# Another order of steps on five engines, and one wait of TensorE moved

## The chip, the cores and the metric

The kernel runs on one core of a Trainium2 chip. The metric is the time of one execution on the device in microseconds (us). The kernel before takes 4313.2 us, the median of three runs (4311.36 to 4319.83 us). On a core five engines work side by side, each through its own stream of instructions: TensorE (PE in the profile, with its weight loads as PEld), VectorE (DVE), ScalarE (ACT), GpSimd (POOL) and SyncE (SP), which here issues the DMAs. They wait for one another by semaphores.

## The reference

The input is 64 sequences of 256 steps with 80 features. `h` holds 252 x 128 values for each:

```python
h = tok(x)                        # taps -2..2 of 80 features -> 128, bias, relu, batch norm over all tokens
h = h + attn0(layernorm(h))       # 8 heads of 16, softmax, +0.1 within 5 steps of the diagonal
h = h + ffn0(layernorm(h))        # 8 experts of 256, exact gelu, the top 2 of a softmax gate
h = h + attn1(layernorm(h))       # linear attention: elu+1 features, causal sums, values of 64
h = h + ffn1(layernorm(h))        # layer norm, causal softmax attention (2 heads, l2 norm), then
                                  # 8 experts of 512, tanh gelu, weighted by a softmax gate
```

All in 32-bit floats; for most products the kernel splits both factors into two 16-bit halves and takes three products for one.

## The kernel before

The 64 sequences are worked in 32 pairs; a pair is 504 tokens, in four tiles of 126. A first stage computes the taps of all pairs and the statistics of the batch norm, and stores the result of each pair in DRAM. After it the pairs go one after the other through the four layers. Their work is cut into steps, written as generators, one per engine and part; a `yield` ends a step, and many steps are empty on a given engine:

- `q` (`softmax_queries_and_keys`, 7 steps): batch norm, layer norm, queries, keys and values of the first attention; queries and keys go to DRAM and come back scattered. q.3 holds the first turn on TensorE (L1378).
- `a` (`softmax_attention`, 32 steps): scores (a.0 to a.7), turn of the maxima (a.8, L1422), scores again and values (a.9 to a.19), projection, layer norm, gate logits, turn of the gates (a.29, L1361) and the product with the output bias (a.30, L1367).
- `l` (`linear_and_causal_attention`, 48 steps): layer norm, turn (l.2, L1346), query and key projection (l.3, L1301 to L1303), values (l.5 to l.7), then l.8 to l.20 with the products of keys and queries (L1543) and those with the values (L1561), turns and projection (l.21 to l.25), turn (l.28, L1346), projection to queries, keys and values (l.29, L1301 to L1303), turn (l.32, L1603), scores (l.33, l.34), turns and values (l.36 to l.40, L1630 and L1641), projection, gate, turn of the gates (l.46, L1361) and bias product (l.47, L1367). On ScalarE l.4 computes the exponentials (L808); on SyncE l.4 sends the terms to DRAM (L457, L461) and scatters them back (L467, L473).
- `h` (`hidden`): one hidden chunk of 128 units of an expert layer: three products on TensorE (L1301 to L1303, 504 columns), the gelu on ScalarE (L886), a cast on VectorE (L1266), the low half on GpSimd (L660). A pair has 16 chunks in the first expert layer and 32 in the second.
- `o` (`output`): the product of a chunk with the second weights, twelve on TensorE (128 columns each), and the weighted sum on VectorE (L1285).

`run_rounds` (L217) sets the order: a start, 30 rounds and an end. Round r holds `a` of pair r+1, `l` of pair r, `q` of pair r+2, the chunks 4 to 31 of the second expert layer of pair r-1, the 16 of the first expert layer of pair r+1, the first four of the second of pair r, and the outputs that belong to them. For each engine and each of start, round and end a string of letters (L159 to L193) says which part takes its next step; `in_order` (L211) walks through it. A string holds 201 letters for the start, 183 for a round and 172 for the end. All semaphore waits stand in the steps, so an engine meets them in the order of its string. The program is unrolled.

TensorE waits once for the small loads (`small_loaded`: bias tables and vectors) ahead of the first step (L1341).

Of the kernel before, what the change touches and what calls it, by code (L numbers as in the profile page):

```python
# [20 lines left out]
TILES = 4  # L21
# [121 lines left out]
def halves_before(kind, p):  # L143
# [15 lines left out]
SP_START = ("qqqqqqqhhhhaaaaaaaaaaaaaaaaaaaaaaaaaaaaaohhaaoalhhqqqooqohohhhqqqhhaaaaaahaaoololhaooaalllolaaaa"  # L159
          "alloooolallllallaaaaaaalllhhaaoaaaaahlollllollqqhhololoqqlhlhlllhlhhhqllhoolllllhqhoohloolhlqool"  # L160
          "lhohholhl")
SP_ROUND = ("lohoholhhllahaaloaolhohhaooaalllllllhohohhhahlaaalolaahhohllolaaolaoohhlaalohlalaoaahalhhhaaooal"
          "hhooalllqhohohhohllolaaaaoloooohhlqqqhhhoahoohohqlholllololqhlhlhhlohholoqloolohhooooll")
SP_END = ("lllllloohlhlohllhlolllooollhhhhooohlhollohllohhhhohlhlllllhhhhohoohhhllohoolllloooolhllllllllhlo"
          "ohlhoolhohhhhhlhhhoolhoooloohhhoohoooooohohhhoooohhhhohhhhohhhohoooooooooooo")
POOL_START = ("qqqqqqqaaaaaaaaaaaaaaaaaaaaaaaaaaaaahhhhhahhhahaqqhqqhhhhhhoqqoqaaaaalalaoolaaoallaolalalalaalal"
          "aaaloololaalaaallllhaaaooalllolohooolhllaoaallolqqhhholhoollllohqlllqhhhhohoohlhlllohqqlohlllloo"
          "hqooholhl")
POOL_ROUND = ("ollhhhllhaloaahaaolhalhllaloahaloaahhahooahlolhallllaahoaahhohaaaahhohloaholohlalahholaallooooll"
          "hqooohlhhlloohoohlolooohooloaaahololhoohhhoallhqqqhhhloohllhlaoolhhhlohloohlolqhqooqlll")  # L170
POOL_END = ("llhllloolhoooooohhlhlhhollllollllllohoolohhllhhhlholllhllhohoohhoholloooolllohhohlolllhhllolllho"
          "hhhhhhhhohhooohoololoooohlhhooohholhholholoohhhhhhohoohhohohhhhooooolohooooo")
# [7 lines left out]
DVE_START = ("qqqqqqqaaaaaaaaaaaaaaaaaaaaaaaaaaaaoaahhhhhaoahqhhqoooohqhqhhooqqoohhoqohhoooolaaaaaallaalllaala"  # L180
          "lallalaaallalaaaallaalllaalaaaallaahaholqlhlllhholqllhhlooolohllhlhqqlhooolllllholhoqohlhqolollh"
          "qhohholhl")
DVE_ROUND = ("laohalohhoalooohloalllhhoahoahohalahallolohhaoollaalohlhlhhalaahllaololhhaaooaalaoahlhaaoholhhoo"
          "olhoalhlaaohqhholhollaoahoaoolhahoolhlohlollqhollqqhholollhahlooqqhlohqloolhhlohhoohlhl")
DVE_END = ("lhlhhohlollollohlohoololohhlhloollllhlohhlolhohlhlllllolhlhoohllooholohollhholohlllhhlollhoolloo"
          "oolhhlllolohhoholhhhlhohooohhhooohhhoooohhhhhoooohhohohhohhhoooohhoohhohoooo")
# [27 lines left out]
def run_rounds(queries_and_keys, first_attention, second_attention, hidden, output, orders):  # L214

    start, middle, end = orders
    last = PAIRS - 1  # L220
# [12 lines left out]
    in_order(end, {
        "l": second_attention(last), "h": each(hidden, chunks_of(1, last - 1)[LAG:] + chunks_of(1, last)),
        "o": each(output, chunks_of(1, last - 1) + chunks_of(1, last))})


def program(nc, x_dram, w_dram, vec_dram, row_dram, b2_dram, out_dram):
    y_dram = nc.dram_tensor("y_scratch", (PAIRS, 128, TOK), F32, kind="Internal").ap()
    term_dram = [nc.dram_tensor(f"terms{i}", (4, 128, TOK), F16, kind="Internal").ap() for i in range(2)]  # L240
    with ExitStack() as ctx:
# [3 lines left out]
        def sem(name):  # L245
            return ctx.enter_context(nc.semaphore(name))
# [117 lines left out]
        small_loaded = sem("small_loaded")  # L364
# [35 lines left out]
        def _(sp):  # L400
# [138 lines left out]
        def _(pool):  # L539
# [128 lines left out]


        @block.scalar  # L670
        def _(act):
# [206 lines left out]
            def hidden(kind, p, c):  # L878
                _, before = chunks_before(kind, p)
                half = halves_before(kind, p)  # L880
                bias = (V_B0, V_B1)[kind] + c
# [4 lines left out]
                nc.scalar.activation(hid[:, c % HIDS], pf[:, c % 2, 0:TOK], func,  # L886
                                     bias=vec[:, bias:bias + 1]).then_inc(F["hid_ready"], 1)

            def output(kind, p, j):
                pass  # L890

            run_rounds(softmax_queries_and_keys, softmax_attention, linear_and_causal_attention, hidden, output,
                       (ACT_START, ACT_ROUND, ACT_END))


        @block.vector
        def _(dve):
# [374 lines left out]
            def output(kind, p, j):  # L1272
# [5 lines left out]
                if m == per - 1:  # L1278
# [5 lines left out]
                    for i in range(TILES):  # L1284
# [5 lines left out]
            run_rounds(softmax_queries_and_keys, softmax_attention, linear_and_causal_attention, hidden, output,  # L1290
                       (DVE_START, DVE_ROUND, DVE_END))


        @block.tensor
        def _(pe):
# [100 lines left out]
            def softmax_attention(p):  # L1396
# [277 lines left out]
            def output(kind, p, j):  # L1674
# [9 lines left out]
                for i in range(TILES):  # L1684
# [60 lines left out]
```

## Time and profile before

| | us |
|---|---|
| median of three runs | 4313.2 |
| run around the profiled execution | 4319.83 |
| span of the profiled execution | 4319.1 |
| TensorE busy | 4066.8 |
| VectorE busy | 3367.6 |
| ScalarE busy | 2784.5 |
| GpSimd busy | 2596.6 |

The span is that of one execution as the hardware profiler saw it. Busy time counts an engine's own instructions, without waits. Products on TensorE overlap: each takes longer than the time between two starts, so starts are what counts for a run of them. Times in a time line are from the span's start. A bracket behind an instruction gives the time for which its engine was idle before it and the instruction that ended this.

### The profile page before, as it was taken

How to read it: one execution, taken by the hardware profiler on the slowest of the kernel's cores; microseconds unless marked ns; L12 is line 12 of the kernel's file. 1: busy time of each engine (PE TensorE's matmuls, PEld its weight loads, DVE VectorE, ACT ScalarE, POOL GpSimd, SP SyncE). 2: the span in 40 equal slices, each digit the busy share in tenths (PEclk: the TensorE clock that was granted, in tenths of full speed). 3: DMA queues.
4: the chain of work that ended last, by engine and by line, in shares of the span. 5: the costliest groups of instructions: out<-in, count | busy, mean ns of one | idle time of the engine just before them, and what ended most of it. 6: DMA issues, size and time to landing. Idle time of an engine off the chain costs nothing.

```text
span 4319.1 us, 104773 instructions
## 1 busy us (share of the span) xinstructions
PE 4066.8 (94%) x41344; PEld 3009.8 (70%) x41344; DVE 3367.6 (78%) x8878; ACT 2784.5 (64%) x4796; POOL 2596.6 (60%) x2494
## 2 busy tenths in 40 slices
PE   7678999999999999999999999999999999999998
PEld 3346777777777777777777777777777777777766
DVE  3357888888888888888888888878888887888876
ACT  3235766666676666667666666766666676666654
POOL 2034666666666666666666666666666666666656
PEclk9779999999999999999999999999999999999999
DMA  4200000011100001110000111000101100010000
GB/s 149 68 27 28 18 18 29 28 30 30 30 19 24 22 28 30 30 30 18 23 23 28 30 30 30 23 26 16 30 28 30 30 23 26 16 30 28 28 16 6
DMA packets 136939, 127.62 MB, mean 30 GB/s; under 512 B 28928, under 2 KB 135360, under 8 KB 136448
## 3 DMA queue, kind: packets, MB, share of 16 engines
q1 hardware_dynamic: 136448, 120.91, 9.6%
q8 instruction: 328, 5.37, 0.5%
q14 instruction: 163, 1.34, 0.1%
HBM read 71.05 MB, written 49.55 MB: 28 GB/s over the span
## 4 chain that ended last, share of the span: by engine, by line
PE 56%; DVE 24%; ACT 6%; POOL 5%; issue 4%; DMA 3%; SPq 2%; ACTq 0%; DVEq 0%; POOLq 0%
PE pf L1301 9%; PE pf L1303 8%; PE pf L1302 8%; PE pa L1561 8%; DVE h L1285 4%; PE pa L1447 3%; DVE hid_hi L1266 3%; PE pa L1543 3%; PE pa L1346 2%; PE pa L1433 2%; POOL inv_norm L650 2%; PE pa L1301 2%; ACT xn L726 2%; PE pa L1641 2%; PE pa L1303 2%
## 5 line engine op out<-in xcount | busy, mean ns | idle before, releaser
L660 POOL TENSOR_TENSOR hid_lo<-hid,hid_hi 128x504 f16<-128x504 f32 x1536 | 1835.5, 1212 | 775.8 <-DVE hid_hi L1266 775.8
L886 ACT ACTIVATE hid<-pf,vec 128x504 f32<-128x504 f32 x1536 | 1014.7, 680 | 505.5 <-PE pf L1303 356.9
L1301 PE MATMUL pf<-w_hi,hid_hi 128*126 128x128 f16 x6144 | 1133.7, 224 | 10.7 <-DVE h L1285 10.2
L1303 PE MATMUL pf<-w_hi,hid_lo 128*126 128x128 f16 x6144 | 1115.8, 221 | 0.0
L1302 PE MATMUL pf<-w_lo,hid_hi 128*126 128x128 f16 x6144 | 1115.4, 221 | 0.0
L1301 PEld LDWEIGHTS pf<-w_hi,hid_hi 128*126 128x126 f16 x6144 | 844.1, 137 | 153.5 <-issue 53.2
L1302 PEld LDWEIGHTS pf<-w_lo,hid_hi 128*126 128x126 f16 x6144 | 843.8, 137 | 28.5 <-issue 0.2
L1266 DVE CAST hid_hi<-hid 128x504 f16<-128x504 f32 x1536 | 845.4, 573 | 8.2 <-ACT hid L886 2.7
L1303 PEld LDWEIGHTS pf<-w_hi,hid_lo 128*126 128x126 f16 x6144 | 845.2, 138 | 0.0
L1285 DVE SCALAR_TENSOR_TENSOR h<-pf,gates,h 126x128 f32<-126x128 f32 x2048 | 574.1, 342 | 155.2 <-PE pf L1303 152.6
L616 POOL TENSOR_TENSOR pt<-pt,band 126x262 f32<-126x262 f32 x512 | 351.2, 707 | 527.6 <-ACT pt L773 527.4
L1301 PE MATMUL pf<-xf_hi,w_hi 128*128 128x504 f16 x1536 | 582.1, 379 | 8.3 <-ACT hid L886 3.0
L1302 PE MATMUL pf<-xf_lo,w_hi 128*128 128x504 f16 x1536 | 578.8, 377 | 0.0
L1303 PE MATMUL pf<-xf_hi,w_lo 128*128 128x504 f16 x1536 | 578.8, 377 | 0.0
L773 ACT ACTIVATE pt<-pa 126x504 f32<-126x504 f32 x512 | 274.7, 589 | 212.3 <-PE pa L1433 211.7
L1561 PE MATMUL pa<-v,pt 126*126 126x65 f32 x3072 | 382.4, 274 | 1.1 <-DVE o L1167 0.9
L1561 PEld LDWEIGHTS pa<-v,pt 126*126 126x126 f32 x3072 | 361.0, 191 | 2.4 <-issue 2.3
L1069 DVE TENSOR_REDUCE minus_max<-pa 126x2 f16<-126x504 f32 x512 | 325.9, 681 | 20.7 <-PE pa L1409 16.6
L886 ACT ACT_TABLE_LOAD x217 | 278.4, 1283 | 6.8
L1303 PEld LDWEIGHTS pf<-xf_hi,w_lo 128*128 128x128 f16 x1536 | 150.3, 98 | 178.0 <-issue 2.2
L1177 DVE TENSOR_TENSOR pt<-pa,causal 126x504 f32<-126x504 f32 x256 | 173.5, 678 | 94.6 <-PE pa L1543 93.3
L1301 PEld LDWEIGHTS pf<-xf_hi,w_hi 128*128 128x128 f16 x1536 | 152.7, 99 | 125.0 <-issue 41.2
(208 smaller groups left out, 7486.8 us busy)
## 6 DMA issues: line engine op xcount, KB each, us to landing
qk_spread<-terms SPq DMA_DIRECT2D x224, 126.0 KB, 2.5
qk_spread<-terms SPq DMA_DIRECT2D x192, 63.0 KB, 2.3
y_scratch<-hid SPq DMA_DIRECT2D x32, 252.0 KB, 2.1
y_in<-y_scratch SPq DMA_DIRECT2D x32, 252.0 KB, 3.2
terms<-qk_hi SPq DMA_DIRECT2D x32, 252.0 KB, 2.5
terms<-qk_lo SPq DMA_DIRECT2D x32, 252.0 KB, 2.6
qk_spread<-terms SPq DMA_DIRECT2D x32, 252.0 KB
terms<-ot_hi SPq DMA_DIRECT2D x32, 252.0 KB, 2.4
```

The source lines that it names most:

```text
L616: nc.gpsimd.tensor_tensor(strip, strip, band[0:TILE], ALU.mult).then_inc(S0["p_band"], 1)
L660: nc.gpsimd.tensor_tensor(hid_lo[:, c % 8], hid[:, c % HIDS], hid_hi[:, c % 8], ALU.subtract).then_inc(hid_lo_done[c % 2], 1)
L773: nc.scalar.activation(pt[0][0:TILE, i % 8], pa0[0:TILE, i % 2, 0:TOK], ACT.Exp, scale=HEAD ** -0.5).then_inc(S0["p_exp"], 1)
L886: nc.scalar.activation(hid[:, c % HIDS], pf[:, c % 2, 0:TOK], func, bias=vec[:, bias:bias + 1]).then_inc(F["hid_ready"], 1)
L1069: nc.vector.tensor_reduce(minus_max[0:TILE, 2 * b:2 * b + 2, hd // 2, 64 * (hd % 2) + MAX_ROW], pa0[0:TILE, i % 3, 0:TOK].rearrange("p (t ...
L1177: nc.vector.tensor_tensor(pt[1][0:TILE, i % 4].rearrange("p (t q) -> p t q", t=4), pa1[0:TILE, 0, 0:TOK].rearrange("p (t q) -> p t q", t=4 ...
L1266: nc.vector.tensor_copy(hid_hi[:, c % 8], hid[:, c % HIDS]).then_inc(F["hid_hi_done"], 1)
L1285: last = nc.vector.scalar_tensor_tensor(h[0:TILE, i], pf[0:TILE, 2, i * D:(i + 1) * D], gates[0:TILE, kind, i, e:e + 1], h[0:TILE, i], ALU ...
L1301: nc.tensor.matmul(out, ah, bh, start=start, stop=False, skip_group_check=skip)
L1302: nc.tensor.matmul(out, ah, bl, start=False, stop=False, skip_group_check=skip)
L1303: return nc.tensor.matmul(out, al, bh, start=False, stop=stop, skip_group_check=skip)
L1561: last = nc.tensor.matmul(pa1[0:TILE, 1, first:first + wide], factors[:, cols(blk)], v1[0:TILE, 2 * b + kt, hd], start=(t == 0), stop=(t = ...
```

## The change

The fifteen strings are replaced by others with the same number of each letter; so every engine takes the same steps, and the steps of each part in the same sequence, but mixed otherwise. The strings of TensorE and ScalarE for a round are shown; those of SyncE, GpSimd and VectorE, and of start and end, change in the same way. TensorE's wait for the small loads moves into `gate_bias2`, in front of the bias product of pair 0 of either layer.

```diff
-ACT_ROUND = ("lhaaohahloaalhlolhhholhahlolahhoalahooaallllooaoahohlllhhhooolaolloaallaahohaalhoalhhhlahaoalhao"
-             "lhohhhoollhooolohoaooalqaaahhalhhlhhllhlolooolooqqqoooloahlllhqloooohhqloohhlqlhholhhll")
+ACT_ROUND = ("aaahhloooahlaloloohhlhhaoohaololoahhaoolhllhhaalllahoalhlholhalllooaqhaahlahaaholoolhoalahhlhaoa"
+             "hqlloaholhqholoooaoohlhaoaloahhaoohohlhllohloolaohllqooolhlhhlqhlhloqoholqhlhlhoolloalh")
...
-PE_ROUND = ("lhhoalhhaoaoloahlohloaoohlhhlaooahlahohalolhalahllaaoolahollhholallhhalaaolaoloahhaolahhlhoohaoo"
-            "laahlhhlaohaoohlolqhoohalolaaohaoohhhoqqqlholhalhloqlolhlolollhhlooqlhhqololhhoohhoolll")
+PE_ROUND = ("lhhalohoaohaloahlohololhqhahhoaloalohahholalhoaloalalaohloolholhalallhhalhalaoalhhaooahlahaholho"
+            "aloqoalhohhooalohqhlalaooaoolhahohahllohoholhlolhlqohlololhlhaqlohlqholqoholhoolhlholol")
...
@@ -1338,7 +1338,6 @@
             pe.wait_ge(w_lo_done, PIECES)
-            pe.wait_ge(small_loaded, 32 + 16 * TILES)
...
             def gate_bias2(a, p):
+                if p == 0:
+                    pe.wait_ge(small_loaded, 32 + 16 * TILES)
                 pe.wait_ge(SS[a]["gate_t_ready"], n(p + 1))
```

Read out, with capital H and O for the second expert layer of the pair before and small h and o for the first of the next pair, parts of TensorE's round are these. The beginning was `l.0 H4 H5 O0 a.0 l.1 H6 H7 a.1 O1 a.2 O2 l.2 O3 a.3 H8 l.3` and is `l.0 H4 H5 a.0 l.1 O0 H6 O1 a.1 O2 H7 a.2 l.2 O3 a.3 H8 l.3`. Up to l.8 it was `H14 O10 H15 a.8 l.8` and is `O9 H14 a.7 H15 H16 O10 l.8 a.8`. Around l.28 it was `l.25 H30 H31 l.26 a.25 O24 h0 a.26 O25 O26 h1 l.27 O27 l.28 q.0 h2 O28 O29 h3 a.27 l.29` and is `l.25 H30 O24 H31 h0 O25 O26 a.25 l.26 O27 h1 q.2 h2 l.27 a.26 l.28 a.27 O28 O29 a.28 O30 O31 l.29`. Up to l.32 it was `O30 l.30 a.28 a.29 O31 h4 a.30 o0 o1 h5 h6 h7 o2 q.1 q.2 q.3 l.31 h8 o3 l.32` and is `h3 a.29 h4 o0 h5 a.30 h6 l.30 l.31 o1 h7 o2 h8 o3 l.32`. The end was `o13 H2 H3 o14 o15 l.45 l.46 l.47` and is `H2 l.45 H3 o14 l.46 o15 l.47` (here H2 and H3 are of the present pair). On ScalarE the steps up to the exponentials were `H7 l.3 O2 l.4 H8` and are `H7 H8 l.4 H9`.

## Rows read from the trace of the kernel before

**Rows 1.** The page: span; then busy time, share and instructions of each engine

```profile
span 4319.1 us, 104773 instructions
...
PE 4066.8 (94%) x41344; PEld 3009.8 (70%) x41344; DVE 3367.6 (78%) x8878; ACT 2784.5 (64%) x4796; POOL 2596.6 (60%) x2494
```

**Rows 2.** Table by stretches: width; five busy times from PE to POOL; PEclk; DMA

```profile
164.00:280.00 116.00, 64.71 (x491) 38.22 (x493) 51.51 (x148) 32.80 (x59) 38.04 (x43) 0.66 0.10 30
280.00:405.00 125.00, 102.33 (x819) 71.09 (x819) 76.02 (x213) 60.43 (x115) 43.20 (x47) 0.82 0.08 22
...
2291.40:2416.60 125.20, 121.44 (x1276) 91.53 (x1275) 103.04 (x277) 85.79 (x148) 80.41 (x79) 1.00 0.10 27
...
4173.00:4319.00 146.00, 124.77 (x1246) 92.44 (x1243) 90.34 (x205) 66.55 (x115) 78.64 (x66) 0.98 0.05 14
```

**Rows 3.** Time line of POOL: marks of the first and the last round

```profile
405.22 0.62 POOL L631 COPY h<-h 126x512 f32<-126x512 f32 x1
...
4170.81 0.62 POOL L631 COPY h<-h 126x512 f32<-126x512 f32 x1
```

**Rows 4.** Time line of PE: end of one round, then l.2 and l.3

```profile
2287.35 0.28 PE L1361 MATMUL pa<-ident,gates 126*128 126x126 f32 x1
2287.98 1.15 PE L1367 MATMUL pa<-b,gate_t 128*126 128x128 f32 x8 [0.35 <-ACT gate_t L736]
2288.97 0.38 PE L1301 MATMUL pf<-xf_hi,w_hi 128*128 128x504 f16 x1
...
2290.24 0.22 PE L1301 MATMUL pf<-w_hi,hid_hi 128*126 128x128 f16 x1
...
2290.87 0.22 PE L1303 MATMUL pf<-w_hi,hid_lo 128*126 128x128 f16 x1
...
2295.14 0.65 PE L1346 MATMUL pa<-ident,xn 126*128 126x126 f32 x4
2297.42 0.38 PE L1301 MATMUL pa<-xt_hi,w_hi 128*128 128x504 f16 x1
```

**Rows 5.** Time line of PE at a.8 and l.8

```profile
2313.84 0.39 PE L1422 MATMUL pa<-ident,minus_max 126*128 126x126 f16 x4 [0.34 <-DVE qk_spread L1075]
2314.07 0.39 PE L1543 MATMUL pa<-qk_spread 128*126 128x126 f16 x4
```

**Rows 6.** Time line of SP: the last scattering DMA of l.4

```profile
2311.31 0.61 SPq L467 DMA_DIRECT2D qk_spread<-terms  x1
```

**Rows 7.** DMA issues of the page: count, KB each, microseconds to landing

```profile
qk_spread<-terms SPq DMA_DIRECT2D x224, 126.0 KB, 2.5
```

**Rows 8.** Time line of PE at l.28, l.29 (first, last), l.32 and l.37

```profile
2367.46 0.65 PE L1346 MATMUL pa<-ident,xn 126*128 126x126 f32 x4 [0.69 <-ACT xn L726]
...
2371.12 0.38 PE L1301 MATMUL pa<-w_hi,xt_hi 128*126 128x384 f16 x1 [0.36 <-DVE xt_lo L1199]
...
2373.25 0.33 PE L1303 MATMUL pa<-w_hi,xt_lo 128*126 128x384 f16 x1
...
2382.97 1.08 PE L1603 MATMUL pa<-ident,v 126*128 126x126 f32 x8 [0.18 <-DVE v L1215]
...
2392.15 0.54 PE L1630 MATMUL pa<-ident,pt 126*126 126x126 f32 x3 [0.77 <-ACT fs L861]
```

**Rows 9.** Waits of PE over the span: total, times, longest

```profile
PE pa L1543 <- DMA qk_spread<-terms: 9.3, 14, 1.1
```

**Rows 10.** The page's groups: busy, mean ns, idle before

```profile
L886 ACT ACT_TABLE_LOAD x217 | 278.4, 1283 | 6.8
```

**Rows 11.** Time line of ACT at an exponential and a gelu

```profile
2322.89 1.07 ACT L773 ACTIVATE pt<-pa 126x504 f32<-126x504 f32 x2 [0.28 <-PE pa L1433]
2323.98 1.28 ACT L886 ACT_TABLE_LOAD   x1
```

**Rows 12.** Time line of DVE at the operand of the first turn

```profile
166.63 0.54 DVE L1036 TENSOR_SCALAR pt<-y_in,bn_scale,bn_shift 128x504 f32<-128x504 f32 x1 [1.64 <-DMA y_in<-y_scratch]
```

**Rows 13.** Time line of PE at the first turn

```profile
168.97 1.09 PE L1378 MATMUL pa<-ident,pt 128*126 128x128 f32 x4 [7.88 <-DMA b<-in_b]
```

More of the change, by code:

```diff
@@ L156 @@
 SPREAD0, SPREAD1 = 6 * 16, 9 * 16
[L159 to L172, printed above, removed]
@@ L173 @@
-ACT_START = ("qqqqqqqaaaaaaaaaaaaaaaaaaaaaaaaaaaaoaohhhoaohaaqhhqqhhqhhhohholhqqqaaaaahhlalaalalllaalaallloaal"
-          "aalaaaoalaalaooollllaalahhloaooaoaaalhooqqllllhhhololhlllhhlooqqholloholhlloolllhlohlqlooqhlhllq"
-          "hoohholhl")
-ACT_ROUND = ("lhaaohahloaalhlolhhholhahlolahhoalahooaallllooaoahohlllhhhooolaolloaallaahohaalhoalhhhlahaoalhao"
-          "lhohhhoollhooolohoaooalqaaahhalhhlhhllhlolooolooqqqoooloahlllhqloooohhqloohhlqlhholhhll")
-ACT_END = ("hhlhhoollolllohhhooolholllhllolohhlllolohlhoohoohllhlollollhloohloohololohlhohlhloohlhllhloooolo"
-          "llolhlhllllolhhlhoooooohhohhhhhhhohhhoolhhohohoohhoohhhooohhohhohoohohoooooh")
@@ L180 @@
[L180 to L186, printed above, removed]
@@ L187 @@
-PE_START = ("qqqqqqqaaaaaaaaaaaaaaaaaaaaaaaaaaaahhhhaahoaahohhqqoqoqhhoohhhhoolooqqhhqoolooooaaaaaalaalllalaa"
-          "laalalalallaalaaalallllaaalaahlhhlaaaaallollhohllhhlqqhhollqlhqooohlhllqhlhololllloolhoolqholoqh"
-          "llohholhl")
-PE_ROUND = ("lhhoalhhaoaoloahlohloaoohlhhlaooahlahohalolhalahllaaoolahollhholallhhalaaolaoloahhaolahhlhoohaoo"
-          "laahlhhlaohaoohlolqhoohalolaaohaoohhhoqqqlholhalhloqlolhlolollhhlooqlhhqololhhoohhoolll")
-PE_END = ("lhlhhhoohlllolhohoooohollhlhllollohlhllhhlolhlolhllhllolllhohoohlloooloolhhholhhhollolollhhllllo"
-          "ololoololhhllhhlhohhohohohhooohhohhooohohhohhooohhhoohohohhhoooohhhhoooooooo")
+SP_START = ("qqoqaaaohqqaahhlqaaahaallqaaaqqaqhaaaahoaaahhhaoahaahhoqahlahaoqaaqahaaqlllolaaolloaaloaaaaoaaao"
+            "hallqohoooaahllaalhalqaalaloqalaoaalahholaoohlhlllaaoloahhhhlqalllhhoallllhlhlqoqollllolllohlhlq"
+            "olhloohho")
@@ new lines @@
+SP_ROUND = ("lhlahaooaahooaollooolhaaooloalohlhlalhlllhhalhahohhaolllolaaalaaqlalahhhalaoaollhlohaollhoqhhaha"
+            "ahollhoohohhooloooolqlhhllhlohahahllhoolaqhhhoaohohhhlaolqhhqqhhhooloohallllolooloooloh")
+SP_END = ("hllhhohloholhlohlllloloolhloollhhlllohohhloolhhhhlhhohohloolhllllllllhhoollhohllhllolooohoololoo"
+          "olhlhlhlolhhloohohhhloohohhhllohhooooohhooohohhhhohooooohohhhoooohhooohooohh")
+POOL_START = ("qoqqqqqaqaaaaaaaaaaaaaaaaaaaqaaahahhhaqahqhhahhhqahhhoahhhqallaaqaaaooalllalalalaalaaqlaoaoaoaao"
+              "aooloalaloqaalalllloaaqahllllaoolhlolaoqhlhloalhloaohohhllhlhqhllqlalllholaqlhoqhhhoahohllllolol"
+              "olhoooolh")
@@ new lines @@
+POOL_ROUND = ("loloaalholhhaoaaohaalholhhalhohqlolhlloaallahohaolhaaoohahohlllaahalhhlohoolalaaolhhooaooallhhqh"
+              "loolooholhhaoololhhlaaolholhlahhhhlholoollqqhlllhooqalhqhoaaahhlllololhoqhhoooooalolhho")
+POOL_END = ("llohlolohlohoolholllhllhohlllhohhlhhllhlolhloolooooohlhllllllooolhhholhollololhhlloohhohhhhoohhh"
+            "loolhlhlolhlhlhoooooohhhoolohlhloohooooooolhholhhohoohhhhooohoohhohohooohhhh")
+ACT_START = ("aaqqaaqqaqoqaqaaaaaaaaaaaaaaaaaqaaaahqhaohhhlhaahhhhqahaqhqhoaqhhqhaoallaallalloolaaalaaaoaaalao"
+             "llaloaqoaaaaallaoolaollqlaahhllqoholohllllaaahohhlololooohallhahhlhllholqollohllqlhqolllqhololhh"
+             "ollhhoolo")
@@ new lines @@
+ACT_ROUND = ("aaahhloooahlaloloohhlhhaoohaololoahhaoolhllhhaalllahoalhlholhalllooaqhaahlahaaholoolhoalahhlhaoa"
+             "hqlloaholhqholoooaoohlhaoaloahhaoohohlhllohloolaohllqooolhlhhlqhlhloqoholqhlhlhoolloalh")
+ACT_END = ("hloollloohollhlhohhhllhlhlooolhlhhohlolohololohloollolhlloolhllhhlololohllhoohhlohloooholhollllh"
+           "llhllololhoohohollhlhhohlhooohohohohoohoohoohohhhohhooohohhhoohhooohhohhohoh")
+DVE_START = ("qqqqqqqaaaaaaaaaaaaaaaaaaaaaoaaaaqaaqaqhhhahhaahoohhohqohoohoqhqhoohaoqhoohooaolaalalalllllaalaa"
+             "aaalaaalaoalllaaaaqallqalaalalaaalahllllhhlhlalhhlholoohlhallolhqhllllolqhhlqoollhoqloollhlohlhq"
+             "lhohlohoo")
@@ new lines @@
+DVE_ROUND = ("loahahohalloohallloahooolohahalhohalaalhooalalohaooahlhlhohlaollllahhalolohqhaahaloaohhalalhhhoo"
+             "alolhaolqoohahoohalhoqollahaaolhahhhoollooolloholhqhhololhlalhlhqhlqolohqoolhhollohohll")
+DVE_END = ("ollhlohlllohloholhohllholohhlllhhllhoolhllolhollhloollolhlloohhlolhoohollhoohlolohololhlllohlhlh"
+           "hololhlhhoolllhhhohlooohhhohooohhhooohooohhhohohooohhhhoohhoohhohhhoooohoooo")
+PE_START = ("qqqqqqqaaaaaaaaaaaaaaaaaaaaaaqaaaqaahahhhhhhqhaooaahhhoqqooohlhohaoqohohqoooooaoaaalllalllaaalal"
+            "qalalaaaalaalalaaaqlalalalaaalhlhahlhallalhlhaqlhholloloollhhhohqhqlloallllhohllolqlloloqollhhlo"
+            "hlhlhoooo")
@@ L196, in chunks_of @@
+PE_ROUND = ("lhhalohoaohaloahlohololhqhahhoaloalohahholalhoaloalalaohloolholhalallhhalhalaoalhhaooahlahaholho"
+            "aloqoalhohhooalohqhlalaooaoolhahohahllohoholhlolhlqohlololhlhaqlohlqholqoholhoolhlholol")
+PE_END = ("hlholhllohllololohhhoohlhlohlhllhoolhllholhllhlolollhllolohhloolhlooollhhhhlohhooollhlohollollol"
+          "lloolohllhhohhoollhlhhhoohhoohohohhohooohhohoohohhohohhohohhooohohhoooohoooo")
 def chunks_of(kind, p):
```

## The prediction

> **What bounds the kernel now.** The page's first part shows TensorE busy for 94% of the span and no other engine above 78% [rows 1]. That share hides how the time is spent, so I went by stages next. The table by stretches has the prologue (164 to 405 us), the rounds and the end as three kinds of work [rows 2]: in the prologue TensorE is busy 64.7 of 116.0 us and then 102.3 of 125.0 us, at a granted clock of 0.66 and 0.82; in a round it is busy 121.44 of 125.20 us at 1.00. One GpSimd copy (L631) runs once a round and marks it: first at 405.22, last at 4170.81 us [rows 3]. That is 30 rounds in 3765.6 us, 125.5 us each, and 148 us of end. So 87% of the span is rounds, and each 0.1 us of a round is worth 3.0 us.
>
> In a round TensorE is the engine that the others must feed. The change issues the same instructions in another order, so TensorE's work in a round stays as it is, and the round changes only by its waits. I read those in the time line of TensorE, where a bracket gives the idle time before an instruction. In the round that starts at 2291.4 us: 0.35 us before the bias product (L1367) [rows 4], 0.34 us within the turn of the maxima (L1422) [rows 5], 0.69 us before the turn L1346, 0.36 us before the projection L1301 and 0.18 us before the turn L1603, and 0.77 us before L1630 [rows 8]. Together 2.69 us. In 14 executions there is also a wait for the scattering DMAs at L1543, 9.3 us in all [rows 9].
>
> **The change, part by part.** A step is written here as in the strings: l.8 is step 8 of the second attention, a.8 of the first, H or h a hidden chunk, O or o an output chunk. Prices of filling work: the two hidden chunks from 2288.97 to 2290.24 us take 0.635 us each; twelve products of an output chunk start 0.057 us apart (2290.24 to 2290.87 us for twelve starts), 0.69 us [rows 4]. For each hand-over I compare the work that TensorE has between sender and receiver, in old and new order, with the time that the chain over the other engines takes.
>
> *l.28 to l.29.* Old: two H and two O (2 x 0.635 + 2 x 0.69 = 2.65 us) and 0.36 us of wait. New: four O, 2.76 us. The wait falls by 0.10 us.
>
> *l.25 to l.28 (first turn of pair r's last part).* New order has five H where the old had four. The wait of 0.69 us falls by 0.64 us.
>
> *l.29 to l.32.* The last product of l.29 ends at 2373.25 + 0.33 = 2373.58 us, 9.4 us before L1603 starts at 2382.97 us [rows 8]. In between ScalarE copies, GpSimd squares, VectorE sums, GpSimd takes the root and VectorE scales, one straight after the other, the last ending as L1603 starts: data, not order, makes this chain, so it keeps its 9.4 us. TensorE's work in it was six O, five H and small steps, by my estimate 1.5 us (4.14 + 3.18 + 1.5 = 8.8 us). In the new order O.30 and O.31 stand ahead of l.29, one H more is here, and q.3 (a turn of 0.5 us) has left: four O, six H, 1.1 us (2.76 + 3.81 + 1.1 = 7.65 us). The wait grows by 8.8 - 7.65 = 1.15 us.
>
> *l.3 to l.8 (queries and keys of the linear attention to DRAM and, scattered, back).* L1301 of l.3 starts at 2297.42 us [rows 4], L1543 of l.8 at 2314.07 us [rows 5]: 16.65 us, 0.34 us of it wait in a.8, so 16.3 us of work. SyncE issues the last scattering DMA at 2311.31 us; with 2.5 us to landing it is in at 2313.8 us, 16.4 us after l.3 [rows 6, 7]. In the new order a.8 (1.05 us without its wait) comes behind l.8 and one H more ahead of it: 16.3 - 1.05 + 0.635 = 15.9 us of work. The sender also gets later: ScalarE has the gelu of chunk H.8 (0.68 us) ahead of the load of the exponential's table that l.4 needs. VectorE's part absorbs some of this; I take 0.7 us of delay, bounds 0 and 1.3 (gelu and about half a table load). L1543 then starts 16.4 + 0.7 = 17.1 us after l.3, and l.8, a.8 and the H are done at 17.1 + 1.05 = 18.15 us; the old order had the same work done at 16.65 + 0.635 = 17.3 us. That is +0.86 us here, some 0.1 more over the rounds with a late landing: +0.95 us, between +0.2 and +1.5.
>
> *o.15 to l.2.* The turn of the gates (l.46) goes ahead of o.15, and the wait of 0.35 us for its copy goes. L1361 starts at 2287.35 and L1346 of l.2 at 2295.14 us, 7.79 us [rows 4], and ScalarE's normalised tiles end just as L1346 starts. VectorE has one cast less in that chain. Work is 0.6 us less, the chain 0.2 us less, l.46 itself is paid ahead: +0.1 us, between -0.3 and +0.5.
>
> *l.34 to l.37, and the exponentials of the first attention among l.8 to l.25.* The 0.77 us before L1630 [rows 8] shrinks; waits of about 0.4 us come at o.6 and at h.12, which are fed by VectorE and GpSimd: -0.1 us, bounds -0.8 and +0.7. The exponentials are late next.
>
> *ScalarE's tables.* The old trace has a load wherever the function changes among exponential and the two gelus (217 of them at the gelu's line [rows 10]); by the strings that is 13 times a round in the old order and 18 times in the new: 5 x 1.283 us = 6.4 us more ScalarE work a round. ScalarE was busy 85.79 of 125.20 us [rows 2], so up to 92.2 us; what hides it is ScalarE's idle time, and what is left falls where TensorE waits for an exponential: 5 of the 18 loads, mostly among steps that have several chunks in hand. Bounds 0 and 6.4 us; I take 0.35 us, near the lower end, since one late load (1.28 us) in the row shown lies between an exponential and a gelu for which TensorE had other steps queued.
> The trace puts a switch at 1.28 us: exponentials run to 2323.96 us by the row, the load starts at 2323.98 us [rows 11]. The Trainium skill, page "ScalarE: Activation LUTs", section "What ACT_TABLE_LOAD costs", adds about 1380 ns of drain to the load. No gap of that size stands in this row. By the page's sum (2.66 us) the five would be 13.3 us of ScalarE time a round, an estimate; its section on table sets, which wants calls with one table put together, speaks against this order.
>
> *Sum of a round:* -0.10 - 0.64 + 1.15 + 0.95 + 0.1 - 0.1 + 0.35 = +1.71 us; 30 rounds +51 us.
>
> *TensorE's wait for the small loads.* The first turn (L1378) waits until 168.97 us, 7.88 us by the bracket, for the bias table; its own operand is written at 166.63 + 0.54 = 167.17 us [rows 12, 13]. Without the wait the turn starts 168.97 - 167.17 - 0.2 = 1.6 us earlier. The new place, the first bias product, comes after all of pair 0's first attention, when the load (in by 168.97 us) has long landed: no price, though all later steps of TensorE would stand behind it otherwise. -1.6 us, or 0 if the prologue has slack there.
>
> *Prologue and end.* SyncE's new start order has the loads of the next pair's rows early; TensorE's has l.8 of pair 0, and its scattering wait, ahead of the exponentials of pair 1, which the old order used partly to fill that wait. By the 16.4 us of the chain this could cost all of a few steps, or, with 51.3 us of the first stretch without TensorE work [rows 2], gain some: +4 us, between -4 and +9. End: 0, within 3. With the -1.6, +2 us.
>
> Total +51 + 2 = +53 us. The profiled execution has a span of 4319.1 us and the 4319.8 us run around it; the median of the three runs is 4313.2 us. On the median: 4313.2 + 53 = 4366 us.
>
> **Rivals.** *Forecast*: new waits at L1603 and L1543 in each round, 4366 us, its own range 4325 to 4405 us (0.3 to 3.0 us a round).
> *Faster*: the sequencing of chunks in the new order covers the waits of the old round, and the delay at l.8 and l.32 is not there, since the chains start earlier than I think. The price is the 2.69 us of waits plus 9.3 / 30 = 0.3 us, at most 3.0 us a round, 90 us; half of it gives 4313 - 45 = 4268 us. For it: four of the waits do get more work ahead of them. Against: the chain into L1603 has no gap to shorten. It decides as soon as the idle time before L1603 stays under 0.2 us and that before L1543 under 0.3.
> *The table loads are exposed*: half of 6.4 us a round stands in TensorE's path, +96 us, 4410 us; all of it, +192 us, 4505 us. Against: TensorE waits for ScalarE mostly at L1346 and L1630, none of them an exponential.
> *Nothing*: gains and losses cancel, and the moved wait alone is left, 4312 us. A difference under 0.2% (8.6 us, 0.29 us a round) is what this kernel's runs cannot tell from none.
>
> **Chances.** Forecast 0.54, faster 0.27, tables 0.08, nothing 0.11. So faster by over 0.2% 0.27, within 0.12 (with a sliver of the forecast), slower 0.61. The range reaches into the faster case down to 4268 us and over half exposed loads to 4420 us.
>
> **What would show it.** Steps between the L631 marks of about 127.2 us; 554 table loads in place of 404; a bracket of over 1 us before L1603 and a DMA wait before L1543 in nearly all rounds; a smaller one before L1346 (l.28) and L1630; the first L1378 at about 167.4 us. The prediction is wrong if the marks stand closer than 125.2 us, or if L1603 no longer waits.

## The result and the profile after

The changed kernel takes 4470.9 us (median of 4 runs, 4464.6 to 4482.2) where the kernel before, run beside it, takes 4312.8: a ratio of 1.0368, 95% interval 1.0349 to 1.0386. That is 158 us slower where 53 were forecast, and outside the range. The two profiled executions (4464.6 and 4319.8 us) lie 144 us apart; all that is read from traces below, and every count of rounds or of low-clock intervals, is of one profiled execution of each kernel.

The page of the profile after: span, busy time by engine, and the group of table loads at the gelu's line (before: [rows 1, 10]).

```profile
span 4462.8 us, 104924 instructions
...
PE 4113.9 (92%) x41344; PEld 3039.7 (68%) x41344; DVE 3374.3 (76%) x8878; ACT 2971.6 (67%) x4946; POOL 2615.6 (59%) x2494
...
L886 ACT ACT_TABLE_LOAD x307 | 393.9, 1283 | 5.5
```

TensorE's share fell, though with the same instructions it was busy 47 us longer. ScalarE has 187 us more: 554 table loads instead of 404. The marks (time line of GpSimd, first and last round, as [rows 3]) say where the time went:

```profile
419.39 0.61 POOL L631 COPY h<-h 126x512 f32<-126x512 f32 x1 [1.33 <-DVE h L1285]
...
4312.68 0.61 POOL L631 COPY h<-h 126x512 f32<-126x512 f32 x1
```

Start to 419.4 us (before 405.2): +14.2. Rounds 3893.3 us, 129.8 each (before 3765.6): +127.7. End 150.1 us: +1.9. The waits of TensorE (us in total, times, longest; in the changed file the lines are one less up to the bias product and one more from there on):

```profile
PE pf L1301 <- DVE h L1285: 79.5, 100, 2.7
PE pa L1360 <- DVE gates L1024: 58.7, 31, 2.0
PE pa L1544 <- DMA qk_spread<-terms: 36.1, 32, 2.6
...
PE pa L1345 <- ACT xn L726: 18.3, 6, 5.4
...
PE pa L1604 <- DVE v L1215: 5.1, 2, 3.8
...
PE pa L1631 <- ACT fs L861: 1.0, 2, 0.5
...
PE pa L1368 <- ACT gate_t L736: 0.4, 1, 0.4
```

The old waits at L1346 (now L1345), L1367 (L1368) and L1630 (L1631) are nearly gone, as predicted (what is left of L1345 stands outside the rounds), and L1543 (now L1544) waits for its DMAs in every round [rows 4, 8, 9]. But L1603 (L1604) hardly waits at all. The prediction named that as a sign that it is wrong. Two others lead, and neither is in the prediction: the turn of the gates (a.29) waits 1.9 us a round for L1024, the last instruction of the top-2 gate on VectorE, and output chunks wait for the weighted sum (L1285) on VectorE. L1024 alone, over the span (min / median / max duration in ns), before:

```profile
L1024 DVE SCALAR_TENSOR_TENSOR gates<-lge,lg x32: 191/191/193, 246.2 to 4130.4; 126x32 f32<-126x32 f32 x32
```

and after:

```profile
L1024 DVE SCALAR_TENSOR_TENSOR gates<-lge,lg x32: 192/1921/1924, 245.0 to 4267.7; 126x32 f32<-126x32 f32 x32
```

The same instruction on the same 126 x 32 values takes ten times as long in 30 of 32 executions. The time lines of one round show what stands beside it. VectorE:

```profile
2450.31 0.42 DVE L1022 TENSOR_REDUCE lge<-ob 126x32 f32<-126x256 f32 x1
2450.77 1.92 DVE L1024 SCALAR_TENSOR_TENSOR gates<-lge,lg 126x32 f32<-126x32 f32 x1
2452.61 0.59 DVE L1285 SCALAR_TENSOR_TENSOR h<-pf,gates,h 126x128 f32<-126x128 f32 x2
```

GpSimd:

```profile
2450.75 1.89 POOL L646 TENSOR_TENSOR o<-v 126x1024 f32<-126x1024 f32 x1 [2.53 <-ACT v L838]
```

TensorE:

```profile
2452.74 0.33 PE L1360 MATMUL pa<-ident,gates 126*128 126x126 f32 x1 [1.95 <-DVE gates L1024]
...
2459.11 0.27 PE L1301 MATMUL pf<-w_hi,hid_hi 128*126 128x128 f16 x1 [0.94 <-DVE h L1285]
```

GpSimd's squares (L646, 1.89 us) begin 0.02 us before L1024, and L1024 ends 0.05 us after them. In the trace of before L646 begins 0.285 us *after* the start of L1024, in every round. In one round (VectorE, GpSimd):

```profile
2373.89 0.19 DVE L1024 SCALAR_TENSOR_TENSOR gates<-lge,lg 126x32 f32<-126x32 f32 x1
...
2374.17 2.00 POOL L646 TENSOR_TENSOR o<-v 126x1024 f32<-126x1024 f32 x1 [3.64 <-ACT v L838]
```

The new order has put one cast (chunk h.2, 0.33 us from start to start) between the first and the second half of the gate (a.27, a.28), and that is enough to lose the race. TensorE then stands idle for 1.95 us before the turn. The 0.94 us before the output chunk o2 at 2459.11 us is not from this: the same 0.94 us stands in every round of the swapped kernel below, in which L1024 is short again.

How long the stretch from l.29 to l.32 is, by the table of stretches (width; busy PE, PEld, DVE, ACT, POOL; PEclk; DMA; GB/s), before:

```profile
2371.10:2383.00 11.90, 11.49 (x113) 8.65 (x113) 10.03 (x25) 6.72 (x11) 8.37 (x5) 1.00 0.09 23
```

and after, in one round, in the next, then in two pieces of that next one (before the turn; later):

```profile
2447.70:2461.20 13.50, 10.46 (x92) 7.03 (x91) 11.39 (x26) 6.75 (x12) 9.57 (x6) 1.00 0.08 20
2574.60:2591.20 16.60, 12.09 (x92) 8.30 (x91) 12.72 (x26) 6.75 (x12) 12.31 (x8) 0.90 0.06 16
2577.20:2579.60 2.40, 0.49 (x3) 0.01 (x1) 2.35 (x3) 2.34 (x3) 1.95 (x2) 1.00 0.01 3
2581.00:2584.40 3.40, 3.40 (x21) 2.78 (x19) 1.25 (x3) 1.17 (x3) 2.36 (x1) 0.50 0.28 76
```

11.9 us have become 13.5 in the first and 16.6 in the second. In the second the granted clock is down: TensorE is busy 0.49 of 2.40 us before the turn, at a clock of 1.00 (2.4 GHz), and from 2581.0 us the clock is 0.50 (1.2 GHz) for a while. The trace after has 27 such intervals within the rounds, 92 us in length together; the rounds before have none. Ten rounds without one take 127.55 us on the mean, 13 rounds with one 130.32, seven with two 131.96. In 19 rounds an interval begins right behind the turn. In these the wait before o2 is 2.40 to 2.70 us, in the other eleven 0.94 us, and seven more intervals begin right behind that longer wait.

### The profile page after: what moved, and what is told of

The parts are those of the page before. It is cut to its first block, busy times and chain, and to the rows that moved or that the text cites. A ratio compares the mean times of both kernels' runs of the same rounds, so it can differ in the third digit from the quotient of the medians.

```text
span 4462.8 us, 104924 instructions
## 1 busy us (share of the span) xinstructions
PE 4113.9 (92%) x41344; PEld 3039.7 (68%) x41344; DVE 3374.3 (76%) x8878; ACT 2971.6 (67%) x4946; POOL 2615.6 (59%) x2494
## 4 chain that ended last, share of the span: by engine, by line
PE 67%; DVE 14%; DMA 5%; ACT 5%; issue 4%; SPq 4%; POOL 1%; DVEq 0%; ACTq 0%; POOLq 0%
PE pf L1301 12%; PE pf L1303 11%; PE pf L1302 11%; PE pa L1562 8%; PE pa L1345 3%; PE pa L1448 3%; PE pa L1544 3%; SPq L473 3%; DVE hid_hi L1266 3%; PE pa L1301 2%; PE pa L1434 2%; PE pa L1303 2%; PE pa L1302 2%; DVE h L1285 2%; DMA qk_spread<-terms 2%
## 5 line engine op out<-in xcount | busy, mean ns | idle before, releaser
L660 POOL TENSOR_TENSOR hid_lo<-hid,hid_hi 128x504 f16<-128x504 f32 x1536 | 1866.0, 1229 | 1159.5 <-DVE hid_hi L1266 1159.5
L886 ACT ACTIVATE hid<-pf,vec 128x504 f32<-128x504 f32 x1536 | 1029.4, 680 | 508.6 <-PE pf L1303 479.6
L1301 PE MATMUL pf<-w_hi,hid_hi 128*126 128x128 f16 x6144 | 1151.3, 225 | 81.2 <-DVE h L1285 79.5
L1303 PE MATMUL pf<-w_hi,hid_lo 128*126 128x128 f16 x6144 | 1135.5, 223 | 0.0
L1302 PE MATMUL pf<-w_lo,hid_hi 128*126 128x128 f16 x6144 | 1134.9, 223 | 0.0
L1302 PEld LDWEIGHTS pf<-w_lo,hid_hi 128*126 128x126 f16 x6144 | 854.1, 139 | 40.5 <-issue 1.6
L1303 PEld LDWEIGHTS pf<-w_hi,hid_lo 128*126 128x126 f16 x6144 | 855.8, 139 | 0.0
L1285 DVE SCALAR_TENSOR_TENSOR h<-pf,gates,h 126x128 f32<-126x128 f32 x2048 | 572.9, 340 | 48.8 <-PE pf L1303 45.2
L1158 DVE TENSOR_SCALAR den<-pa 126x4 f32<-126x4 f32 x256 | 40.7, 159 | 258.1 <-PE pa L1562 255.4
```

What stands on the lines that cost most here:

```text
L1285: last = nc.vector.scalar_tensor_tensor(h[0:TILE, i], pf[0:TILE, 2, i * D:(i + 1) * D], gates[0:TILE, kind, i, e:e + 1], h[0:TILE, i], ALU ...
L1301: nc.tensor.matmul(out, ah, bh, start=start, stop=False, skip_group_check=skip)
L1302: nc.tensor.matmul(out, ah, bl, start=False, stop=False, skip_group_check=skip)
L1303: return nc.tensor.matmul(out, al, bh, start=False, stop=stop, skip_group_check=skip)
```

## The experiments

Each was timed beside the kernel before (4318.6, 4321.5 and 4320.0 us in the three groups); ratios are to it, with their 95% intervals. "Start", "rounds" and "end" are read from the marks.

**The wait alone.** The old strings, TensorE's wait moved:

```diff
-            pe.wait_ge(small_loaded, 32 + 16 * TILES)
...
+                if p == 0:
+                    pe.wait_ge(small_loaded, 32 + 16 * TILES)
```

> The kernel before with its own strings; only TensorE's wait for the small loads is moved. By the prediction the first turn (L1378) starts 1.6 us earlier, so the time is 0 to 2 us under the kernel before (4311 to 4313 us). A rival: in the profile of the changed kernel this turn starts at 162.3 us instead of 169.0, so the move alone could give up to 6.7 us (4306 us). Either way nothing of the 158 us comes from here.

Measured 4315.5 us, ratio 0.9999 (0.9988 to 1.0010): no difference that can be told. The earlier start of the first turn in the changed kernel was mostly the stage before it, which ends some us earlier or later from run to run.

**The cast out of the way.** In the changed kernel, one swap in VectorE's string:

```diff
-"...q.2 O30 l.28 l.29 a.27 h2 a.28 a.29 O31..."   # VectorE's round, read out
+"...q.2 O30 l.28 l.29 a.27 a.28 h2 a.29 O31..."
```

> The changed kernel, where VectorE does the top-2 gate (a.28) before the cast of chunk h.2 (0.33 us) instead of behind it; nothing else. Theory, collision: in 30 rounds the gate's last instruction (L1024) is issued 0.02 us after GpSimd has begun its squares (L646) and takes 1.92 us instead of 0.19; TensorE is idle for 1.95 us at a.29, VectorE is late for the rest of the stretch up to l.32, and in 19 of 30 rounds the granted clock falls to 0.50 for 3.4 us. The cast away, L1024 ends 0.1 us before L646 begins: 0.19 us, no idle before L1360, l.29 to l.32 near 9.5 us instead of 13.4 or 16.5, hardly a low-clock interval in the rounds; rounds of 123.5 to 126 us, 4290 to 4360 us. Rival, the prediction's sum: data make the chain to l.32, so the idle time moves from a.29 to l.32 and the round stays at about 127 us, 4385 to 4400 us. Rival, table loads: nothing changes, 4470 us.

Measured 4353.6 us, ratio 1.0085 (1.0070 to 1.0101): some 120 of the 158 us were in that one swap. L1024, and the stretch from l.29 to l.32:

```profile
L1024 DVE SCALAR_TENSOR_TENSOR gates<-lge,lg x32: 191/191/195, 246.0 to 4159.7; 126x32 f32<-126x32 f32 x32
```

```profile
2392.80:2404.60 11.80, 10.36 (x89) 6.84 (x87) 10.64 (x26) 6.65 (x11) 8.84 (x6) 1.00 0.08 22
```

L1024 is back at 191 ns, the stretch at 11.8 us, rounds at 126.1, and two low-clock intervals are left in the rounds. The table loads are still 554.

**The same swap in the old order.** It was to provoke the collision there:

```diff
-"...l.29 a.27 O29 a.28 h2 O30 a.29..."   # VectorE's round of the kernel before
+"...l.29 a.27 O29 h2 a.28 O30 a.29..."
```

> The kernel before, where VectorE does the cast of chunk h.2 ahead of the top-2 gate (a.28) instead of behind it; nothing else. Theory, collision: L1024 now starts some 0.05 us after GpSimd's L646 has begun, takes 1.9 us, and TensorE's turn of the gates (L1360 or L1361) waits about 1.7 us in each round; with what VectorE then has late, +1 to +2 us a round, and if the clock falls in some rounds up to 2 us more: 4345 to 4430 us. Rival, the new mixture of TensorE's steps is what costs: one cast of 0.33 us moved by one step changes nothing, 4308 to 4318 us.

Measured 4323.6 us, ratio 1.0011 (1.0001 to 1.0020). It didn't provoke it: L1024 came 0.21 us later, not 0.33, and L646 still begins 0.08 us behind its start; L1024 takes 192 ns (VectorE, GpSimd, one round):

```profile
2375.14 0.19 DVE L1024 SCALAR_TENSOR_TENSOR gates<-lge,lg 126x32 f32<-126x32 f32 x1
...
2375.22 1.89 POOL L646 TENSOR_TENSOR o<-v 126x1024 f32<-126x1024 f32 x1 [3.65 <-ACT v L838]
```

So it became the control: later by 0.21 us on VectorE costs 0.1%, and the rival was not yet ruled out.

**The collision made in the old order.** One comparison of the gate once more, into a spare buffer:

```diff
+                nc.vector.tensor_tensor(spare[0:TILE], other, mine, ALU.is_gt)
                 nc.vector.tensor_tensor(over[0:TILE], other, mine, ALU.is_gt)
```

> The kernel before, all strings as they were; in each top-2 gate one comparison is computed once more into a spare buffer, 0.34 us on VectorE, so that the gate's last instruction (L1024) comes not 0.285 us before GpSimd's squares (L646) but some 0.05 us behind their start. The run before this one, with a delay of 0.21 us on VectorE, left L1024 0.08 us ahead of L646 and cost 0.1% at most: that is the control. Theory, collision (a lock between the two engines): L1024 takes about 1.9 us, TensorE's turn of the gates waits 1.5 to 1.9 us, every round is 1 to 2 us longer, and if the clock then falls as in the changed kernel up to 5 us: 4350 to 4460 us. Rival, the length of L1024 comes from something else in the new order (its operands' banks, a late semaphore): L1024 stays at 0.19 us, the turn is 0.1 to 0.3 us late, 4318 to 4330 us.

Measured 4390.4 us, ratio 1.0160 (1.0141 to 1.0179). L1024 (L1026 in this file) over the span, and TensorE's turn in a round:

```profile
L1026 DVE SCALAR_TENSOR_TENSOR gates<-lge,lg x32: 191/1886/1891, 248.6 to 4199.8; 126x32 f32<-126x32 f32 x32
```

```profile
2412.01 0.33 PE L1363 MATMUL pa<-ident,gates 126*128 126x126 f32 x1 [1.90 <-DVE gates L1026]
```

The 0.13 us more that put L1024 behind the squares' start cost some 65 us. L1024 takes its 1.9 us and the turn waits, with strings that are all old, so the rival (something else in the new order) is out. Rounds are 127.9 us, with 14 low-clock intervals. Here the collision is nearly all of it: the 16 rounds without an interval take 127.52 us on the mean, 2.0 us over before, and the 14 with one 128.30 us, only 0.8 us more.

**The squares in two halves.** In the changed kernel GpSimd does L646 as two instructions:

```diff
-                nc.gpsimd.tensor_tensor(squares[0:TILE], qkv[0:TILE, :, 0:2 * D], qkv[0:TILE, :, 0:2 * D],
-                                        ALU.mult).then_inc(S1["sq_ready"], 1)
+                for half in (slice(0, 2), slice(2, 4)):
+                    last = nc.gpsimd.tensor_tensor(squares[0:TILE, half], qkv[0:TILE, half, 0:2 * D],
+                                                   qkv[0:TILE, half, 0:2 * D], ALU.mult)
+                last.then_inc(S1["sq_ready"], 1)
```

> The changed kernel with GpSimd's squares (L646, 1.9 us) computed by two instructions of half the size. Theory, collision as a lock held for one GpSimd instruction: L1024 gets in between the halves and takes about 1.0 us, the idle time before a.29 falls to about 1.0 us and the low-clock intervals become fewer: 4380 to 4430 us. Rival, the two engines share a rate or L1024 waits for all of GpSimd's queue: L1024 stays at 1.9 us or more, 4460 to 4480 us.

Measured 4381.2 us, ratio 1.0136 (1.0117 to 1.0154). L1024 (here L1026), and the two squares:

```profile
L1026 DVE SCALAR_TENSOR_TENSOR gates<-lge,lg x32: 192/1073/1073, 248.2 to 4188.3; 126x32 f32<-126x32 f32 x32
```

```profile
2416.50 2.04 POOL L647 TENSOR_TENSOR o<-v 126x512 f32<-126x512 f32 x2 [2.52 <-ACT v L840]
```

L1024 now waits for one half: 1073 ns instead of 1921. Rounds are 126.6 us, with no low-clock interval at all. So L1024 is held for one GpSimd instruction, whole, and with 1.1 us of idle time before the turn (32.9 us in 30 rounds) the clock stays up. Against the changed kernel the 30 rounds are 95 us shorter, while the first mark stands 12 us later in this trace.

**TensorE's gap filled.** In the changed kernel h4 and o0 ahead of a.29:

```diff
-"...O31 l.29 h3 a.29 h4 o0 h5 a.30..."   # TensorE's round
+"...O31 l.29 h3 h4 o0 a.29 h5 a.30..."
```

> The changed kernel, where TensorE takes h4 and o0 ahead of the turn of the gates (a.29) instead of behind it; L1024 still meets GpSimd's squares. Theory: L1024 keeps its 1.9 us, but TensorE's idle time before a.29 falls from 1.95 to some 0.5 us, and it is this idle time that the clock answers to: the low-clock intervals (27 in the rounds, 3.4 us each) all but vanish, and with them some 70 us; with 1 us a round of what VectorE has late left over: 4370 to 4400 us. Rival: the clock falls whatever stands in that gap, or the low intervals come from the idle time before o2: 4440 to 4475 us.

Measured 4465.2 us, ratio 1.0343 (1.0312 to 1.0373). A miss: o0 itself waits for VectorE, which has the sum of O31 queued behind L1024, so the gap moved by one chunk and got longer (2.3 us). The waits for L1285 show it (79.5 us in the changed kernel):

```profile
PE pf L1301 <- DVE h L1285: 141.4, 130, 2.4
```

It doesn't tell whether a filled gap would have kept the clock up. But the low-clock intervals moved with the gap: 16 of the 20 in these rounds begin between 0.1 us before and 1.3 us behind its end.

**ScalarE's exponentials first.** On the swapped kernel (4353.6 us):

```diff
-"...l.3 O4 O5 H7 H8 l.4 H9..."   # ScalarE's round
+"...l.3 O4 O5 H7 l.4 H8 H9..."
```

> The changed kernel with the top-2 gate ahead of the cast (4353.6 us), and on ScalarE the exponentials of l.4 ahead of the gelu of chunk H.8, as the old order had them. Theory of the prediction: this gelu delays the terms by 0.7 us (0 to 1.3), and l.8 waits that much longer; so the wait before L1543 falls by 0.5 to 1.2 us a round, 4318 to 4340 us. Rival: the chain to l.8 is set by the DMAs and SyncE, the gelu is absorbed by VectorE: within 5 us of 4353.6.

Measured 4341.3 us, ratio 1.0047 (1.0031 to 1.0062); rounds fall from 126.08 to 125.60 us, as long as before the change (125.52). The wait for the scattering DMAs is down from 38.5 us to:

```profile
PE pa L1544 <- DMA qk_spread<-terms: 24.9, 32, 1.4
```

The prediction's mechanism, at 0.48 us a round instead of 0.7 (0.34 against the 28 rounds of the swapped kernel without low clock, 125.94 us). The round still has 18 table loads and runs as long as the old one with 13.

**a.8 ahead of l.8**, on the swapped kernel:

```diff
-"...H16 O10 l.8 a.8 l.9..."   # TensorE's round; VectorE's: a.7 l.8 a.8 becomes a.7 a.8 l.8
+"...H16 O10 a.8 l.8 l.9..."
```

> The changed kernel with the top-2 gate ahead of the cast (4353.6 us), and a.8 ahead of l.8 on TensorE and VectorE, as the old order had it. Theory of the prediction: the wait at l.8 (about 1.3 us) is filled by the 1.05 us of a.8, so a round loses 0.7 to 1.05 us: 4322 to 4333 us. Rival: a.8 first makes VectorE late for l.8's followers and the wait moves on: within 8 us of 4353.6.

Measured 4352.8 us, ratio 1.0075 (1.0050 to 1.0099). The rival's time was right: the wait ahead of l.8 is filled, and it moves on. The engine was another one: l.9, now straight behind l.8, waits 0.7 us a round for ScalarE's work on the products of l.8 (L825), a wait that the swapped kernel doesn't have.

```profile
PE pa L1544 <- ACT pt L825: 20.1, 30, 0.7
```

**All repairs with the old start:**

> All repairs at once: the top-2 gate ahead of the cast, l.4 ahead of H.8 on ScalarE, a.8 ahead of l.8, a.3 behind H.8 on TensorE (fills 0.5 us of wait for the maxima), o.0 and o.1 ahead of the cast of h.6 on VectorE (o.2 waits 1.1 us for o.1; 0.3 us expected), and the old start. From 4353.6 us: l.8 -1.3, a.3 -0.5, o.2 -0.3 us a round, together -63 us, start -4 to -8: 4282 to 4290 us, under the kernel before. Rival: each wait filled comes back at the next hand-over, and the old order's 125.2 us a round is the floor: 4310 to 4325 us.

Measured 4326.5 us, ratio 1.0017 (1.0004 to 1.0029). A miss by some 40 us: rounds 125.9 us, no better than the exponentials alone. As its rival said, each wait that was filled came back at the next step: 0.59 us before l.3, 0.67 before l.9, and 0.33 of the wait before o2 at l.32.

**The old start, the new rounds; and the reverse.**

> The changed kernel with the start strings of the kernel before on all five engines; rounds and end as changed, and the wait moved. The first mark (L631) stood at 405.2 us before and 419.4 us after the change, though the first turn of pair 0 was 6.7 us earlier: some 20 us lost within the start. With the old start the mark comes at 398 to 405 us and the time falls by 14 to 21 us, to 4450 to 4457 us; rounds stay at 129.8 us. If the start's loss were only shifted into the rounds, the time stays within 5 us of the changed kernel.

Measured 4466.5 us, ratio 1.0341 (1.0315 to 1.0368), not to be told from the changed kernel: the mark came 8 us earlier, but the rounds had 32 low-clock intervals instead of 27 and were 10 us longer.

> The kernel before with the new start strings alone (and TensorE's wait moved); rounds and end are old. The start of the changed kernel is 14 us longer by its mark, of which the mark's own place in the new round may be some. If the new start costs what the marks say: 4328 to 4335 us; if the first rounds take the loss back: 4315 to 4322 us.

Measured 4335.3 us, ratio 1.0035 (1.0023 to 1.0047): some 15 us, with rounds as before (125.5). In the second part of the start (before 125.0 us at a clock of 0.82 [rows 2]) it reads:

```profile
280.00:422.90 142.90, 110.44 (x804) 78.34 (x805) 76.38 (x206) 60.04 (x114) 44.72 (x48) 0.75 0.07 20
```

TensorE is idle for 32 of 143 us there instead of 23 of 125, at a lower clock.

**An attempt at a faster version**, from the swapped kernel with the exponentials first, old start and end:

```diff
-"...o1 h7 o2 h8 o3 l.32 h9 l.33 o4 l.34..."   # TensorE's round
+"...o1 h7 h8 o2 o3 h9 l.32 o4 l.33 l.34..."
```

> An attempt at a version under both: the changed round with the top-2 gate ahead of the cast and l.4 ahead of H.8 on ScalarE (rounds of 125.6 us), the start and end of the kernel before, and on TensorE h8 ahead of o2 and h9 ahead of l.32, o4 ahead of l.33, to fill the 1.1 us that o2 waits. If the fillings hold: 0.3 to 0.8 us a round under the kernel before, 4296 to 4312 us. Rival, as in the two fillings before: the chain over VectorE and GpSimd to l.32 keeps its length and l.33 is late instead: 4315 to 4330 us.

Measured 4406.5 us, ratio 1.0206 (1.0185 to 1.0226): worse than its rival said. o2 no longer waits as long, but behind l.32 too little is left for TensorE: the time from l.32 to the next step grows by 1.6 us, with 1.4 us of idle time before o4, and 17 of the 19 low-clock intervals in the rounds begin 1.9 to 4.1 us behind it. No version ran faster than the kernel before.

## Why the prediction was wrong

The direction was right, the main term was missing. The sum went wrong at its premise "TensorE's work in a round stays as it is, and the round changes only by its waits", as it was used in the step l.29 to l.32, where "data, not order, makes this chain". I priced the other engines' instructions at their old durations, whatever stood beside them. L1024 was not in any term: its 1.9 us stood at nothing. Nor does TensorE's work stay as it is. The table of stretches from the first mark to the last, before and after:

```profile
405.22:4170.81 3765.59, 3642.97 (x38156) 2743.71 (x38157) 3086.26 (x8234) 2569.77 (x4433) 2409.95 (x2309) 1.00 0.09 26
...
419.39:4312.68 3893.29, 3687.18 (x38176) 2768.23 (x38177) 3095.71 (x8236) 2757.09 (x4583) 2431.91 (x2309) 0.99 0.09 25
```

Its busy time in the rounds grew by 44 us, about half of the 92 us that it ran at half the clock. The sum had no term for the clock.

The 127.7 us in the rounds divide like this. The new order without the collision: the 28 rounds of the swapped kernel without a low interval take 125.94 us, 0.42 over before, 12.6 us in 30 rounds. The collision itself: 127.55 - 125.94 = 1.61 us, 48.3 us. What goes with the low clock: 13 x (130.32 - 127.55) + 7 x (131.96 - 127.55) = 66.9 us. Some 39 of these are TensorE's longer work in those rounds and some 28 its waits, the longer one before o2 above all. That the collision is the cause was shown from both sides, by removing it, halving it and making it. That the clock falls because TensorE stands idle there fits all of it (27 intervals with the collision, none with half of it, 14 in the old order with it, and intervals that move with the gap where h4 and o0 stand ahead of the turn), but no run changed the idle time alone.

Point by point, by the mean steps of TensorE in the swapped kernel, where the collision is out of the way:

- *l.29 to l.32*: without the collision the chain does keep its length (11.87 us from the start of l.29, before 11.86), and TensorE's missing work shows as waits: 0.18 us before a.29, 0.57 before o0 and 1.10 before o2, where VectorE is late, not before L1603; the old waits at h6 and o3, 0.64 together, went. That is +1.2 us, predicted +1.15: right in size, wrong in place.
- *l.3 to l.8*: predicted +0.95; the wait ahead of l.8 grew by 1.33 us and a.8 lost 0.39, together +0.94.
- *l.25 to l.28*: predicted -0.64; the wait ahead of l.28, 0.82 us by starts, is gone. *l.28 to l.29*: predicted -0.10; the wait ahead of l.29, 0.52 us by starts, is gone, and 0.27 came behind l.28, together -0.25.
- *o.15 to l.2*: predicted +0.1; l.46 lost 0.52 us, o.15 gained 0.19.
- *l.34 to l.37*: predicted -0.1; -0.93 at h11, +0.85 at l.36 and l.38.
- Not in the sum: 0.49 us of wait between h9 and l.33 went too, and 0.50 came before a.3. The first could have been read: TensorE waits for ScalarE at L1614 (the scores of l.33) in nearly every pair before, and the 2.69 us of waits in the prediction leave this one out, so they were some 3.3 us.

```profile
PE pa L1614 <- ACT pt L843: 19.2, 31, 0.8
```

- All together, without the collision the round came to +0.56 us on the mean, not +1.71: this part of the sum was too high by two thirds, though its two largest terms held.
- *Table loads*: 18 a round as counted. No run priced them alone, but a round that has all 18 takes 125.60 us, one with 13 takes 125.52, and in the rounds of the changed kernel TensorE's waits for ScalarE are 8.5 us in all, 0.28 a round. So the rival in which 3.2 to 6.4 us of a round are exposed is out.
- *The wait for the small loads*: the operand is written at 161.60 + 0.54 us (time line of VectorE) and the turn starts at 162.40 (TensorE), 0.26 us later where it was 1.80 [rows 12, 13]; 1.5 us, as predicted, and too little for the timed runs.

```profile
161.60 0.54 DVE L1036 TENSOR_SCALAR pt<-y_in,bn_scale,bn_shift 128x504 f32<-128x504 f32 x1 [1.54 <-DMA y_in<-y_scratch]
```

```profile
162.40 1.09 PE L1379 MATMUL pa<-ident,pt 128*126 128x128 f32 x4 [6.23 <-DVE pt L1036]
```

- *Prologue*: predicted +4 (-4 to +9) without the wait; some 15 us measured with the start strings alone. The reason that it gave (pair 1 stands behind pair 0's scattering) was not tested; idle time and a lower clock came together there (0.75, before 0.82), and the clock was in no term.

The trace of before held a warning that was not read. VectorE's L1004, one instruction in the code, ends the softmax of the gate in either layer, on 126 x 32 values both times. Over the span (min / median / max in ns):

```profile
L1004 DVE TENSOR_TENSOR lg<-lge,lmax x32: 191/192/193, 243.8 to 4128.0; 126x32 f32<-126x32 f32 x32
L1004 DVE TENSOR_TENSOR gates<-lge,lmax x32: 191/708/712, 397.3 to 4268.6; 126x32 f32<-126x32 f32 x32
```

In the 30 long executions the second starts some 0.6 us behind the start of a low half on GpSimd (L660) and ends 0.05 us behind its end, as L1024 did behind the squares. It was paid in nearly every pair of the old order, where TensorE waited for it only once, 0.5 us. The Trainium skill, page "SBUF — State Buffer", section "Who interferes with whom", says that a VectorE instruction with two inputs in SBUF contends with a GpSimd instruction that reads SBUF, and that whichever issues second is blocked until the other is done. The traces agree for VectorE's side: 192 ns when L1024 comes first, 1921 when it comes second, 1073 behind half the work. For GpSimd's side they show nothing: L646 took 1.89 us as first and, in the control run, as second. By that rule the place of each such pair in the two strings would have been a term of the sum.

## What to carry to other kernels

When an order is rewritten, look up in the old trace which pairs of VectorE and GpSimd instructions stand close to each other in time, with their distance: a short instruction on the path that wins its race by 0.3 us is a hidden term as large as the GpSimd instruction it races. A price for a lost microsecond on TensorE must ask for the clock, and for what stands behind: in the new order rounds that were 48 us late from the collision lost 67 us more with the low clock, in the old order 60 us of collision came with only 11. And a gap can be filled only with work that doesn't wait for the engine that is late.

## What the hardware showed that was not expected

VectorE's instruction of 126 x 32 values was held for the whole of GpSimd's instruction, not slowed: 0.02 us behind its start cost 1.73 us, 0.08 us ahead of it nothing. An instruction of VectorE that reads PSUM was not held: the weighted sum (L1285), with one of its two tiles in PSUM, has the same median whether a GpSimd instruction is running at its start or not (342 and 341 ns, 1478 and 570 executions before). And idle time and granted clock came in a chain: of 30 rounds with the same instructions and the same 1.95 us of idle time before the turn, 19 had the clock fall right behind it; in these the next wait, before o2, grew from 0.94 us to 2.40 to 2.70, and behind it the clock fell seven times more. What decides between the 19 and the eleven stays open.
